# Encoder attention on one core: the value products of two rounds in one batch, and a third buffer of exponentials

## The reference

```python
def layer(h, p):
    q = (h @ wq + bq_).reshape(Bx, Sx, H, HD).transpose(0, 2, 1, 3)
    k = (h @ wk + bk_).reshape(Bx, Sx, H, HD).transpose(0, 2, 1, 3)
    v = (h @ wv + bv_).reshape(Bx, Sx, H, HD).transpose(0, 2, 1, 3)
    scores = jnp.einsum('bhqd,bhkd->bhqk', q, k) * scale
    scores = scores * smask
    a = jax.nn.softmax(scores, axis=-1)
    att = jnp.einsum('bhqk,bhkd->bhqd', a, v)
    att = att.transpose(0, 2, 1, 3).reshape(Bx, Sx, Dx) @ wo + bo_
    h = _ln(h + att, g1, be1)
    ff = jax.nn.gelu(h @ w1 + b1_, approximate=False) @ w2 + b2_
    h = _ln(h + ff, g2, be2)
    return (h, None)
```

## Time and profile before

| | |
|---|---|
| three runs | 4402.39, 4403.99, 4404.39 us (median 4403.99) |
| profiled execution, span | 4402.3 us; its own whole time is not listed apart |
| busy: TensorE, VectorE, ScalarE, GpSimd | 3675.8, 2637.4, 1814.6, 910.3 us |
| TensorE's granted clock, mean | 0.906 |
| encoder | the first 2010 us or so |
| one layer's attention (the third) | from 706 to 941 us |

### The profile page before, as it was taken

One profiled execution on the slowest core, in us unless ns is written; L12 is line 12 of the kernel. 1 busy time (PEld: TensorE's weight loads), 2 busy tenths in 40 slices (PEclk: granted clock), 3 DMA queues, 4 the chain that ended last, 5 costly groups with the idle time before them and its releaser, 6 DMA issues. The chain is left out here.

```text
span 4402.3 us, 70735 instructions
## 1 busy us (share of the span) xinstructions
PE 3675.8 (83%) x27255; PEld 2535.9 (58%) x27255; DVE 2637.4 (60%) x6733; ACT 1814.6 (41%) x2861; POOL 910.3 (21%) x1164
## 2 busy tenths in 40 slices
PE   5998998998998998985999978677756666997996
PEld 3665665665666666664777745455635433443664
DVE  4866866866867857854222239888668562113663
ACT  2553554554554554552333335322223122331443
POOL 2323333333332333321000001000100230003321
PEclk8998998998998998997999988799867667997997
DMA  5514514414514524501000000000000000003330
GB/s 131 121 47 110 117 44 119 116 44 110 123 47 105 120 56 97 120 26 44 1 1 1 1 15 1 0 1 0 1 6 0 5 0 27 0 0 83 96 86 24
DMA packets 156739, 224.99 MB, mean 51 GB/s; under 512 B 16158, under 2 KB 136350, under 8 KB 139422
## 3 DMA queue, kind: packets, MB, share of 16 engines
q10 hardware_dynamic: 19656, 107.37, 11.0%
q1 hardware_dynamic: 136750, 113.11, 9.4%
HBM read 156.84 MB, written 60.82 MB: 49 GB/s over the span
## 5 line engine op out<-in xcount | busy, mean ns | idle before, releaser
L801 DVE TENSOR_REDUCE enc_mx<-psum 128x2 f32<-128x512 f32 (+1 forms) x1152 | 756.1, 685 | 169.5 <-PE psum L491 167.0
L983 ACT ACTIVATE enc_e<-psum 128x1024 f32<-128x1024 f32 (+1 forms) x768 | 580.4, 808 | 435.8 <-PE psum L512 325.0
L491 PE MATMUL psum<-enc_ks,enc_qs 80*128 80x128 bf16 (+1 forms) x3072 | 465.8, 255 | 89.7 <-DVE enc_mx L801 54.0
L512 PE MATMUL psum<-enc_qs,enc_ks 83*128 83x256 bf16 (+1 forms) x3072 | 386.0, 251 | 43.0 <-ACT enc_e L983 31.8
L491 PEld LDWEIGHTS psum<-enc_ks,enc_qs 80*128 80x128 bf16 x3072 | 224.5, 100 | 217.4 <-DVE enc_mx L801 106.8
L523 PE MATMUL psum<-enc_e,enc_v 128*32 128x256 f32 (+1 forms) x6144 | 332.7, 334 | 0.0
L512 PEld LDWEIGHTS psum<-enc_qs,enc_ks 83*128 83x128 bf16 x3072 | 262.2, 99 | 81.6 <-ACT enc_e L983 40.8
L1854 ACT ACTIVATE moe_act_h<-psum 128x512 f32<-128x512 f32 x288 | 169.4, 598 | 305.9 <-PE psum L1728 305.7
L1750 PEld LDWEIGHTS psum<-par_s,moe_act_h 128*128 128x128 f32 x2304 | 269.7, 192 | 30.1 <-issue 28.5
L1817 DVE SCALAR_TENSOR_TENSOR moe_acc<-psum,moe_gates,moe_acc 128x128 f32<-128x128 f32 x256 | 72.1, 345 | 345.3 <-PE psum L1750 345.3
L1750 PE MATMUL psum<-par_s,moe_act_h 128*128 128x128 f32 x2304 | 272.6, 275 | 0.0
(11 more groups left out here) (473 smaller groups left out, 7034.0 us busy)
## 6 DMA issues: line engine op xcount, KB each, us to landing
enc_qs<-q_pieces ACTq DMA_DIRECT2D x234, 192.0 KB
enc_ks<-k_pieces ACTq DMA_DIRECT2D x234, 192.0 KB
k_pieces<-enc_pieces SPq DMA_DIRECT2D x240, 128.0 KB, 2.0
q_pieces<-enc_pieces SPq DMA_DIRECT2D x144, 128.0 KB, 2.2
enc_qs<-q_pieces SPq DMA_DIRECT2D x54, 192.0 KB
enc_ks<-k_pieces SPq DMA_DIRECT2D x54, 192.0 KB
rope_qs<-q_pieces ACTq DMA_DIRECT2D x39, 192.0 KB
rope_ks<-k_pieces ACTq DMA_DIRECT2D x39, 192.0 KB
```

The lines of the kernel that those rows point to most:

```text
L491: last = T_.matmul(p1[f % 2][:, i * kw:(i + 1) * kw], qs[0:KEYED, slot, h, j * P:(j + 1) * P], ks[0:KEYED, slot, h, 0:kw], start=True, sto ...
L512: last = T_.matmul(p2[ch][:, g], ks[0:SCORED, slot, 4 * T + g, ch * P:(ch + 1) * P], qs[0:SCORED, slot, 4 * T + g, 0:n], start=True, stop= ...
L801: V.tensor_reduce(mx[:, u % 2, j * HEADS + h0:j * HEADS + h0 + n], p1[f % 2].rearrange("p (h k) -> p h k", h=n), AX_X, ALU.max)\
L983: A.activation(e_of(T, ch), p2[ch], ACT.Exp, scale=HD ** -0.5).then_inc(s_e, 1)
```

## The change

The value products of rounds 0 and 1 of a sequence are both done in its round 2, and those of rounds 2 and 3 both in round 0 of the next sequence (behind round 3 of the last sequence of a layer). The exponentials have three buffers, counted through all rounds of all layers, and `expo` waits for the value product three back. Nothing else moves, and no instruction is added.

```diff
-        e = sb("e", [P, 2, HT * (S + P)])
+        e = sb("e", [P, 3, HT * (S + P)])
...
-        e_of = lambda T, ch: (e[:, T % 2, 0:HT * S].rearrange("p (g q) -> p g q", g=4), e[:, T % 2, HT * S:].rearrange("p (g q) -> p g q", g=4))[ch]
+        e_of = lambda n, ch: (e[:, n % 3, 0:HT * S].rearrange("p (g q) -> p g q", g=4), e[:, n % 3, HT * S:].rearrange("p (g q) -> p g q", g=4))[ch]
...
-                        if T:
-                            values(layer, u, T - 1)
-                        elif u:
+                        if T == 2:
+                            values(layer, u, 0)
+                            values(layer, u, 1)
+                        elif T == 0 and u:
+                            values(layer, u - 1, 2)
                             values(layer, u - 1, 3)
...
+                values(layer, SEQS - 1, 2)
                 values(layer, SEQS - 1, 3)
...
             def expo(layer, u, T):
-                if 4 * u + T >= 2:
-                    act.wait_ge(s_pv, at(layer, SEQS * HT, 4 * u + T - 1))
+                n = at(layer, SEQS * HT, HT * u + T)
+                if HT * u + T >= 3:
+                    act.wait_ge(s_pv, n - 2)
                 for ch in range(JT):
                     act.wait_ge(s_p2, at(layer, 128, 8 * u + 2 * T + ch + 1))
-                    A.activation(e_of(T, ch), p2[ch], ACT.Exp, scale=HD ** -0.5).then_inc(s_e, 1)
+                    A.activation(e_of(n, ch), p2[ch], ACT.Exp, scale=HD ** -0.5).then_inc(s_e, 1)
```

More of the change, by code:

```diff
@@ L522, in values @@
                     for g in range(4):
-                        last = T_.matmul(o[T // 2][32 * g:32 * g + 32, T % 2, 0:n], v[:, u % SLOTS, ch, 4 * T + g], e_of(T, ch)[:, g],
+                        last = T_.matmul(o[T // 2][32 * g:32 * g + 32, T % 2, 0:n], v[:, u % SLOTS, ch, 4 * T + g], e_of(at(layer, SEQS * HT, HT * u + T), ch)[:, g],
                                          start=(ch == 0), stop=True, skip_group_check=(ch > 0))
```

## The result

The changed kernel takes 4449.68 us, the median of four runs (4448.09 to 4457.91); beside it the kernel before takes 4404.19 (four runs, 4402.39 to 4414.24). The ratio is 1.0103, with a 95% interval of 1.0088 to 1.0113: 1% slower. The forecast was 4408 with a range to 4427. The profiled execution is the slowest of the four (span 4455.6 us, against 4402.3 before), so of its 53 us about 8 are its own; up to the last round of the encoder's last attention it has 43.8 more (1952.65 against 1908.84), and I look for those. Two executions among those of the experiments, one of 9557 us (e1) and one of 7977 us (the kernel before), lie far off all others and don't enter the ratios.

A forecast was written before the change was run, and what follows sets the result against it. TensorE's saving was taken to lie under VectorE and be given back at the layers' ends. Six layers at +0.3 (+1.8) and five starts (+2.0), together +3.8 on the median 4403.99, gave 4407.8; range 4390 to 4427.

The forecast's parts named there:

- The seam: Inside a doubled batch: saves 0.20 us of changeovers (0 to 0.22), so it holds TensorE 1.47 us instead of 0.79.
- rival D: In a doubled batch: the seam pays the same changeover, 1.58 us plus entry; +7 us, 4415; chance 0.12.
- the changeover ahead of a batch: On TensorE before a batch's first load: taken as 0.10 us, between 0 and 0.11, though no row shows it.
- The even sequence: Sequences with query and key projections: masked sum unmoved, round 1's exponentials 0.57 us late; 14.14 instead of 14.06, +0.08.
- The odd sequence: Odd sequences: round 1's fill and reduction come earlier, VectorE's 7.42 us run on from there; -0.30 us each.
- no wait, but 0.08 to spare: Odd sequence, scores of round 2: exponentials at 6.40 allow them at 7.47, TensorE gets there at 7.55.
- Rival C: Round 1's exponentials late behind moved sums and six DMA issues, round 3 repays nothing: even +0.51 us; 4430, chance 0.23.
- Round 3 gives back 0.89: Round 3 without its batch: returns 0.89 us, 0.79 for the batch and 0.10 for the changeover ahead.
- Ends of a layer: Sequences 12 to 15 of each layer: +0.5, -0.14, +0.41 and +0.6 us.
- the walk of 14: Sequence 14: round 1's exponentials 0.68 us later, round 2's scores 0.41 late, sequence 15 starts later: +0.41.
- Layer starts: Sequence 1 of layers 1 to 5: doubled batch behind ScalarE's stall at low clock; +0.4 us each, +2.0 together.

The follow-up runs named there:

- e1: Kernel after with only the products of rounds 0 and 1 doubled, in round 2; those of rounds 2 and 3 single again: 4400.81 us, ratio 0.9979.
- e5: Kernel after with a filler batch of unread value matmuls in odd round 3 and the six loads on SyncE's queue: 4393.01 us, ratio 0.9957.
- e3: Kernel after with a filler batch of eight value matmuls, result unread, in round 3 of odd sequences (42 places): 4430.31 us, ratio 1.0053.
- e9: Kernel after with the same kind of unread filler batch in round 3 of even sequences instead (48 places): 4466.80 us, ratio 1.0140.
- e4: Kernel after with the six loads of each sequence issued from SyncE's queue instead of ScalarE's: 4420.83 us, ratio 1.0021.
- e7: Kernel before with the six loads of each sequence issued from SyncE's queue instead of ScalarE's: 4412.67 us, ratio 1.0002.

## Why the prediction was wrong

*The seam.* Right: 1.44 us to the next matmul, forecast 1.47, against 1.58 for two single ones; rival D is out. That saves 0.14, where the forecast's 1.47 had 0.11 for this seam; the changeover ahead of a batch, the other 0.10 of its 0.20, no row shows. One changeover less agrees with the rule of the Trainium skill (TensorEngine Tiling (Array Packing), Key Properties) that a change of mode drains TensorE; the size is this trace's.

*The even sequence.* Right where nothing disturbs it: 14.08 us (forecast 14.14), masked sum at 3.80, exponentials of round 1 at 6.14 (6.17), fills at 9.67 and 11.55 (9.70 and 11.61). That these late exponentials are what keeps it from gaining is shown by e5: on time, it takes 13.59. But 10 of the 30 even sequences are 0.65 to 2.7 us longer than before, 15.8 us together; the sum had 30 x 0.08 = 2.4 for all. Nine of the ten are those with the low clock.

*The odd sequence.* Right in the regular place, 14.75 us (forecast 14.90): VectorE's work from that reduction on is 7.41 us, forecast 7.42, and only the reduction starts earlier than I had it, at 7.34 instead of 7.48. But the 30 odd sequences together are 0.2 us longer than before, where the sum had them 9.0 shorter. Wrong is the step "no wait, but 0.08 to spare". It walked the six issues behind the moved sums and not the wait ahead of them. In the sequence that I read the first load is issued at 822.94, 3.25 us in; the last store of key pieces had landed at 822.92, so even there the store set it and not the sums. In all 30 odd sequences of the kernel before it is so, and the first load is issued between 3.23 and 5.38 us in, in the median at 4.10. After the change the exponentials behind it start at up to 8.78, against my 6.40.

Rival C (chance 0.23, 4430) had the late exponentials, and its price of 26 us is near to e3, where the clock hardly falls (0.53%, 23 us). That the sums agree is in part luck: of C's terms the odd sequences that gain nothing and the ends (11; 9.5 in e3) came true, but its even sequences (15) cost 3.1 in e3's regular part together with the odd ones, and the rest of e3's loss lies at the layers' starts and in the feed-forward parts.

*Round 3 gives back 0.89.* This is the step that failed without a rival. The batch of odd round 3 was not only 0.79 us of TensorE's time: it stood between two waits for VectorE (0.81 and 0.35), and without it they are 0.51, 0.20 and 0.87 with little work between. I had read the clock's price where it was already low (1.50 for a batch of 0.86 in sequence 1), and put the clock at nothing everywhere else: I did not ask where TensorE's emptier queue would bring it down anew. It brought it down in sequences 2 to 15 for 65 us, where the kernel before has none. By e3 this is worth 0.5% of the time, half of what was lost.

*Ends of a layer.* The sum was 1.37 per layer, 8.2 us; measured 23.1, with sequence 15 taken to the first matmul of the feed-forward part. Sequences 13 and 15 came as forecast (0.0 and +3.7 us over six layers, forecast -0.8 and +3.6), 12 and 14 cost 9.1 and 10.3 (forecast 3.0 and 2.5). In e3, where the clock stays up here, they are 4.9 and 2.1, so the walk of 14 was right, its start was not: in three of the four layers where it is long, it inherits the low clock from the end of 13. Timeline of the third layer, where the clock held, answering to the earlier trace rows:

```profile
948.89 1.51 ACT L987 ACTIVATE enc_e<-psum 128x1024 f32<-128x1024 f32 x2 [1.07 <-PE psum L512]
949.97 0.88 PE L512 MATMUL psum<-enc_qs,enc_ks 83*128 83x256 bf16 x8 [0.51 <-ACT enc_e L987]
...
955.26 0.83 PE L512 MATMUL psum<-enc_qs,enc_ks 83*128 83x256 bf16 x8 [1.21 <-DMA enc_qs<-enc_turned_max]
```

*Layer starts.* Forecast +2.0 in all; sequences 0 and 1 have +3.3, the feed-forward parts +3.3, and sequence 2 +6.0, 5.1 of it in the two layers where the clock is low there. The scores of sequence 1 wait 31.3 us over layers 1 to 5, 28.3 before; answering to the earlier trace rows:

```profile
762.53 1.51 ACT L987 ACTIVATE enc_e<-psum 128x1024 f32<-128x1024 f32 x2 [9.32 <-issue]
763.61 1.03 PE L512 MATMUL psum<-enc_qs,enc_ks 83*128 83x256 bf16 x4 [7.08 <-ACT enc_e L987]
...
766.07 2.79 PE L523 MATMUL psum<-enc_e,enc_v 128*32 128x256 f32 x32
```

The doubled batch falls wholly in the low clock here, at 2.79 us, 1.29 more than the single one before (1.50), within the 0.68 to 1.5 that I had allowed. The feed-forward parts scatter between 85.9 and 90.3 us over all kernels and layers, in both directions, and I did not test them.

Shown by experiments: that the batch missing from odd round 3 costs 0.5% (e3, with e9 as control), that the loads ahead of the exponentials cost 0.8% (e4), and that both cures together take back more than the whole loss (e5). That the 0.5% comes through the granted clock, and not through some other effect of the filler, is read from the traces: undisturbed sequences are as long in e3 as in the kernel after, and in both kernels and e4 the long even sequences are those with a low clock. The clock was not set apart from everything else. Nor is it known why the last store of key pieces lands in some 2.0 us in one sequence and 4.0 in another. Sequence 12 is 2.2 us longer than before in e5 over the six layers, within the 3.0 that the forecast had for it.

## What to carry to other kernels

A batch that is moved away from between two waits leaves longer waits with less work between them; look there in the new trace whether the granted clock still holds, in every layer and not in one. When something is put ahead of DMA issues in an engine's queue, take the time of those issues from all their occurrences, with the spread, and look which of their waits ended last; and keep work that the bound engine waits for out of a queue that can block on a DMA. If half of a change keeps the gain and the other half the loss, try them apart before judging the idea: here the same idea gives 1.0103, and with the loads moved and round 3 filled 0.9944.

## What was not expected of the hardware

Work whose result nobody reads made the kernel faster, by 0.5% (ratio 1.0103 to 1.0053), with 42 batches of it. And no long wait stood where the clock fell: ahead of the transposes at 278.15 TensorE had waited 0.51, 0.20 and 0.87 us, and the transposes, scores and value products behind ran at the lower level; at 858.58 the same three waits left the clock at 1.00. What decides between the two these runs don't tell.

The six DMA issues of a sequence on ScalarE's queue took 0.30 us for the first and 0.38 to 0.39 for each other, 2.4 us with their gaps (833.89 to 836.27), in which the engine does no exponentials. The same six on SyncE's queue take 2.3 us; there they stand ahead of the maxima's DMA, and the traces show a cost of it at the start of a layer (e5, e7).
